# Third edge stage: five of 403 groups fetched row by row through SyncE instead of by GpSimd's gathers

## The reference

```
h = silu(emb @ mlp_w0 + mlp_b0); h = silu(h @ mlp_w1 + mlp_b1)
w = (h @ mlp_w2 + mlp_b2).reshape(-1, 4, MUL)
ss = xs[senders]; vv = xv[senders]
m0 = w[:, 0] * ss
m1 = w[:, 1][:, :, None] * ss[:, :, None] * Y1[:, None, :]
m2 = w[:, 2][:, :, None] * vv
m3 = w[:, 3] * (jnp.einsum('emc,ec->em', vv, Y1) / SQ3)
msg = segment_sum(concatenate(m0, m3, m1, m2), receivers)
```

## Time and profile before

| | |
|---|---|
| median of three runs | 11160.38 us (11138.41 to 11165.17) |
| profiled execution | 11197.17 us, span 11195.4 us |
| busy in the span | PE 7512.2 us, DVE 6853.5, ACT 4365.1, POOL 7061.2 |
| third edge stage | about 5899 to 8612 us |
| DMA in the span | 16 engines, mean 76 GB/s |

### The profile page before, as it was taken

The page is one execution under the profiler, slowest core; times in us unless marked ns, Lnnn a source line. Parts: engine busy times, 40 slices in busy tenths (PEclk is TensorE's granted clock), DMA queues, the critical chain, the costliest instruction groups (busy, mean ns, idle before and its releaser), DMA issues. The chain is left out here.

```text
span 11195.4 us, 158258 instructions
## 1 busy us (share of the span) xinstructions
PE 7512.2 (67%) x45679; PEld 5676.2 (51%) x45679; DVE 6853.5 (61%) x18737; ACT 4365.1 (39%) x7367; POOL 7061.2 (63%) x6167
## 2 busy tenths in 40 slices
PE   1333333335899998998956777777777677777775
PEld 1322322333666666666645666666666344444443
DVE  3555555566677777666655666666666444444445
ACT  1111121121667776666621111111111566666664
POOL 3666666662688888888855555556554655555554
PEclk5555555556889999999977888888888788888887
DMA  4434434442666666777761111111111111111111
GB/s 118 110 96 105 111 98 104 101 97 65 103 106 106 107 106 109 109 109 109 110 117 46 43 43 43 43 42 43 42 42 46 45 43 44 44 44 45 44 44 43
DMA packets 1068830, 846.48 MB, mean 76 GB/s; under 512 B 404136, under 2 KB 907183, under 8 KB 1067542
## 3 DMA queue, kind: packets, MB, share of 16 engines
q0 software_dynamic: 360512, 407.88, 20.9%
q1 hardware_dynamic: 676812, 313.54, 12.7%
q10 hardware_dynamic: 30652, 115.04, 3.1%
HBM read 696.14 MB, written 139.60 MB: 75 GB/s over the span
## 5 line engine op out<-in xcount | busy, mean ns | idle before, releaser
L1474 POOL DMA_INDIRECT sums<-sumrows,index x1460 | 2458.1, 1684 | 694.3 <-issue 348.9
L1623 POOL DMA_INDIRECT rows<-table,index x1612 | 1583.8, 982 | 1128.8 <-DVE mid L1680 582.1
L679 POOL DMA_INDIRECT rows<-table,index x1612 | 1609.3, 998 | 1015.9 <-issue 692.0
L1873 POOL DMA_INDIRECT ACC<-table,index x1472 | 1398.4, 950 | 1129.2 <-DVEq L1998 615.1
L1650 DVE TENSOR_TENSOR ACC<-ACC,psS 128x256 f32 x1612 | 674.6, 418 | 792.1 <-PE psS L1714 471.2
L1714 PEld LDWEIGHTS psS<-hot,mid 128*128 128x128 f32 x6448 | 1042.9, 230 | 57.7 <-issue 3.0
L1714 PE MATMUL psS<-hot,mid 128*128 128x128 f32 x6448 | 1032.2, 313 | 2.7 <-DVE mid L1680 2.3
L2045 PE MATMUL psG<-limbs,pickA 128*128 128x384 bf16 x4060 | 902.1, 355 | 159.4 <-issue 102.7
L1910 ACT ACTIVATE pickA<-apart,K 128x512 bf16<-128x512 bf16 x1015 | 721.2, 711 | 717.2 <-remote 475.0
L1966 DVE TENSOR_TENSOR pickD<-ACC,psK 128x512 bf16<-128x512 f32 x700 | 459.9, 682 | 746.4 <-remote 545.4
L1421 PE MATMUL psB<-pickD,limbs 128*128 128x512 bf16 (+1 forms) x2964 | 824.5, 391 | 81.5 <-DVE pickD L1288 77.0
(11 more groups left out here) (349 smaller groups left out, 15303.0 us busy)
## 6 DMA issues: line engine op xcount, KB each, us to landing
win<-table SPq DMA_DIRECT2D x1612, 64.5 KB
srow<-src_f SPq DMA_DIRECT2D x365, 256.0 KB
HN<-rel_f ACTq DMA_DIRECT2D x102, 512.0 KB
relB<-rel_f ACTq DMA_DIRECT2D x102, 512.0 KB
rows<-table,index POOLq DMA_INDIRECT x3224
er<-limbs SPq DMA_DIRECT2D x1632, 3.0 KB
ACC<-table,index POOLq DMA_INDIRECT x1472
sums<-sumrows,index POOLq DMA_INDIRECT x1460
```

The source lines that it names most:

```text
L679: nc.gpsimd.indirect_dma_start(out=rows[:, r, k, :], out_offset=None, in_=table0[:, :], in_offset=bass.IndirectOffsetOnAxis(ap=index[:, n ...
L1474: nc.gpsimd.indirect_dma_start(out=sums1[u][:, :], in_=sums[:, n % 2, u, :], in_offset=None, compute_op=ALU.add, out_offset=bass.IndirectO ...
L1623: nc.gpsimd.indirect_dma_start(out=rows[:, n % R, u, :], out_offset=None, in_=table2[:, :], in_offset=bass.IndirectOffsetOnAxis(ap=index[: ...
L1873: nc.gpsimd.indirect_dma_start(out=rows[:, n % R, u, :], out_offset=None, in_=table3[:, :], in_offset=bass.IndirectOffsetOnAxis(ap=index[: ...
```

## The change

SP takes over the rows of five groups, numbers 75, 150, 225, 300 and 375 (BYSP); POOL keeps the 398 others (QUICK), over the same four buffers, counted in its own order. SP's loop is written out over the 403 groups. After the load of base it issues its share of the request in hand: 73 steps (SPREAD) for the 512 rows of one group, in 64 batches of 8 (PACE). Before the first batch it loads the 512 source numbers into one partition (`listP`) and waits for them; from the third request on it first waits until the group that last used the buffer is done. A batch reads eight numbers into registers and issues eight DMAs of one row each. The rows go to two buffers of their own (`rowsP`) with a semaphore each, for which DVE waits at those five groups. DVE's other work reads `taken` in place of `rows`. Three semaphores and two tiles are new.

```diff
--- before.py
+++ after.py
@@ -1584,6 +1584,12 @@
                     R = 4
                     last = EDGE_GROUPS - 1
                     index = sb("index2", [P, T], I32)
+                    SPREAD, PACE = 73, 8
+                    BATCH = U * P // PACE
+                    BYSP = [SPREAD + 2 + (SPREAD + 2) * k for k in range(5)]
+                    QUICK = [n for n in range(EDGE_GROUPS) if n not in BYSP]
+                    rowsP = sb("rowsP2", [P, 2, U, C])
+                    listP = sb("listP2", [1, U * P], I32)
                     rows = sb("rows2", [P, R, U, C])
                     base = sb("base2", [2 * NB, R, 2 * P])
                     h1 = sb("h1_2", [P, 2 * P])
@@ -1598,33 +1604,55 @@
                     (s_h0, s_h1, s_h1p, s_h2, s_hot, s_w, s_mid, s_sum, s_free, s_dot, s_dot3, s_q1) = (sem(n + "_e2") for n in (
                         "s_h0", "s_h1", "s_h1p", "s_h2", "s_hot", "s_w", "s_mid", "s_sum", "s_free", "s_dot", "s_dot3", "s_q1"))
                     s_rows = gathered2
+                    s_listP, s_rowsP = sem("s_listP_e2"), sem("s_rowsP_e2", 2)
                     s_index, s_base = sem("s_index_e2"), sem("s_base_e2", R)
                     with nc.Block() as block:
                         @block.sync
                         def _(sp):
                             sp.dma_start(index[:, :], a["src_cols"]).then_inc(s_index, 16)
 
-                            def load(n, g, r):
+                            def eight(b):
+
+                                _, at = nc.values_load_multi_w_load_instructions(
+                                    listP[0:1, b * PACE:b * PACE + PACE], engines=(sp.engine,), min_val=0, max_val=NPAD - 1,
+                                    skip_runtime_bounds_check_because="a src is a node number, and padding edges have one too")
+                                return at
+
+                            for n in range(EDGE_GROUPS):
                                 sp.wait_ge(s_mid, n + 1)
-                                sp.dma_start(base[:, r, :], basis[bass.ds(n * 2 * NB, 2 * NB), :]).then_inc(s_base[r], 16)
-
-                            ring(sp, EDGE_GROUPS, R, load)
+                                sp.dma_start(base[:, n % R, :], basis[n * 2 * NB:(n + 1) * 2 * NB, :]).then_inc(s_base[n % R], 16)
+                                k, step = divmod(n, SPREAD)
+                                if k < len(BYSP):
+                                    for b in range(BATCH * step // SPREAD, BATCH * (step + 1) // SPREAD):
+                                        if b == 0:
+                                            if k > 1:
+                                                sp.wait_ge(s_mid, BYSP[k - 2] + R + 1)
+                                            sp.dma_start(listP.rearrange("o (t p) -> o t p", t=U), a["src_cols"][:, BYSP[k] * U:BYSP[k] * U + U].rearrange("p t -> t p").unsqueeze(0),
+                                                         allow_slow_non_contiguous=True).then_inc(s_listP, 16)
+                                            sp.wait_ge(s_listP, 16 * k + 16)
+                                        at = eight(b)
+                                        for i in range(PACE):
+                                            u, p = divmod(b * PACE + i, P)
+                                            sp.dma_start(rowsP[p:p + 1, k % 2, u, :], table2[bass.ds(at[i], 1), :]).then_inc(s_rowsP[k % 2], 16)
+                            sp.wait_ge(s_index, 16)
+                            for r in range(2):
+                                sp.wait_ge(s_rowsP[r], 16 * U * P * uses(len(BYSP), 2, r))
                             for r in range(R):
                                 sp.wait_ge(s_base[r], 16 * uses(EDGE_GROUPS, R, r))
 
                         @block.gpsimd
                         def _(pool):
                             pool.wait_ge(s_index, 16)
-                            for n in range(EDGE_GROUPS):
-                                pool.wait_ge(s_mid, n + 1)
+                            for f, n in enumerate(QUICK):
+                                pool.wait_ge(s_mid, QUICK[f - R] + R + 1 if f >= R else 1)
                                 pool.nop(nofuse=True)
                                 for u in range(U):
                                     at = n * U + u
                                     nc.gpsimd.indirect_dma_start(
-                                        out=rows[:, n % R, u, :], out_offset=None, in_=table2[:, :],
-                                        in_offset=bass.IndirectOffsetOnAxis(ap=index[:, at:at + 1], axis=0)).then_inc(s_rows[n % R], 16)
+                                        out=rows[:, f % R, u, :], out_offset=None, in_=table2[:, :],
+                                        in_offset=bass.IndirectOffsetOnAxis(ap=index[:, at:at + 1], axis=0)).then_inc(s_rows[f % R], 16)
                             for r in range(R):
-                                pool.wait_ge(s_rows[r], 16 * U * uses(EDGE_GROUPS, R, r))
+                                pool.wait_ge(s_rows[r], 16 * U * uses(len(QUICK), R, r))
 
                         @block.scalar
                         def _(act):
@@ -1653,9 +1681,16 @@
 
                                 s = r % 2
                                 one_hots(hot[:, s, :, :], n).then_inc(s_hot, 1)
-                                dve.wait_ge(s_rows[r], 16 * U * g + 16 * U)
-                                scalars = rows[:, r, :, 0:F]
-                                vectors = rows[:, r, :, F:C].rearrange("p u (c k) -> p u c k", c=3)
+                                if n in BYSP:
+                                    k = BYSP.index(n)
+                                    taken = rowsP[:, k % 2, :, :]
+                                    dve.wait_ge(s_rowsP[k % 2], 16 * U * P * (k // 2 + 1))
+                                else:
+                                    f = QUICK.index(n)
+                                    taken = rows[:, f % R, :, :]
+                                    dve.wait_ge(s_rows[f % R], 16 * U * (f // R) + 16 * U)
+                                scalars = taken[:, :, 0:F]
+                                vectors = taken[:, :, F:C].rearrange("p u (c k) -> p u c k", c=3)
                                 along = unit[:, bass.ds(n * U, U), :].unsqueeze(3).to_broadcast([P, U, 3, F])
                                 m1 = mid[:, s, :, 2 * F:5 * F].rearrange("p u (c k) -> p u c k", c=3)
                                 m2 = mid[:, s, :, 5 * F:8 * F].rearrange("p u (c k) -> p u c k", c=3)
```

## The result

The changed kernel takes 11392.94 us (11387.45 to 11399.67) against 11162.77 us, a ratio of 1.021 with a 95% interval of 1.0192 to 1.0227: 230 us slower, where no change was forecast and 11195 us was the upper end. Its profiled execution took 11387.45 us, span 11385.7.

What follows compares the result with a forecast made beforehand. Third edge stage bound by handovers between PE, ACT and DVE, not POOL's gathers. POOL's relief 0, SP's added work 0, semaphores 0.1 us, bounds -25.6 and +22: 11160 us, no measurable change, range 11125 to 11195.

Steps and rivals of the forecast that it cites:

- bounds of 0 and 22 us for the list: SP's load of 512 source numbers, five times: delay of base costs 0, at most 22 us.
- that idle time hides all of it: SP, third edge stage: 332 us of added work per request of 489, hidden by 1837.8 us of waits; cost 0.
- a wrong releaser: DVE's 260.4 us at line 1650, named as waiting for a load of HN; which semaphore was left open.
- rival B: SP's row loads in each step become the bound, base late, PE waits: 12535 us, mild case 11300; chance 0.07.
- a ring of handovers: Third edge stage: PE, ACT and DVE wait for each other, no engine full; DVE's sums wait 471.2 us, 393 times.
- its own 0.82: Rival B's threshold on SP: it decides above 0.82 us per row; every 0.1 us over costs 256 us.
- the 5.13 at most: SP's step with a batch takes 5.13 us of 6.70; a batch delays the next base by at most that.
- the cover of 9.3 us: SP's base loads: used 13.4 us after issue, issue and landing at most 4.1 us, so 9.3 us spare.
- Rival A: POOL sets the pace where waits do not show: 25.6 us go, 11135 us, -0.23%; chance 0.06.
- C: List or batches on SP make base late beyond the bound, at five places: 11200 us; chance 0.05.
- D: SP's request is not overlapped because each row's DMA is awaited; excluded by the change's text, no chance of its own.
- my 0.6: SP's load of eight row numbers into registers: 0.3 to 0.6 us expected, 0.6 taken.

Runs made afterwards that it cites:

- e6: The changed kernel unaltered, beside the kernel before in a session at the lower level: 15 us faster.
- e20: The changed kernel's list, register loads and row DMAs replaced by 7680 posts, POOL gathering all 403 groups, upper level: 156 us (1.52%) slower than the kernel before.
- e8: The changed kernel with 5632 row DMAs at fixed addresses, no register work, POOL gathering all groups, upper level: 216 us slower than the kernel before.
- e14: Same kernel as e20 (7680 posts, POOL gathering all 403 groups), at the lower level: 0.07 to 0.10% slower than the kernel before.

## Why the prediction was wrong

**Right.** The row loads' medians, 37 + 29 + 228 ns. At the lower level they stood (3.15 - 0.228) / 7 = 0.42 us apart (e6's timeline, forecast 0.516); in the changed kernel itself the median distance within a batch is 0.65 us and the mean 0.70, more than forecast. PE never waited for base beyond the first, the rows came in time, the list cost two waits, 8.2 us of SyncE's and nobody else's; bounds of 0 and 22 us for the list hold with 0. DVE's instructions and POOL's time went as forecast (1583.8 to 1562.6 us, idle up by 246 us).

**The step that failed** is in the part on SyncE: "that idle time hides all of it". I priced SyncE's work by what SyncE has to spare and by who waits for its results. The runs show a third way to pay: at this level, while SyncE issues, the others are released late, and it need not be row loads. e20 shows it with nothing but 7680 posts that nobody reads, 156 us, and e8 with 5632 DMAs at fixed addresses and no register work, 216 us. So the cost I put at 0 was the 230 us. A range by SyncE's spare time could not contain it. How the 230 us divide among the register loads, the register operations, the moves and the DMAs is not shown: the register work was not tried alone at this level.

**Signs that stood in my own rows.** I left a wrong releaser open, 260.4 us at DVE with the name of a load of HN, and passed over the 784.6 us that ACT waited for "remote" in the same view. I saw a load of median 333 ns with single ones of 17853 ns and a stretch of 1.36 us each, and put it down to the load's own 128 pieces, in rival B. The move beside it, with no piece at all, went to 1405 ns in the same stage; had I asked for the line's moves, I would have seen a stop that is not the DMA's. At the lower level the 17.8 us DMA is still there (17789 ns in e6) and the slow moves are not: two things stood under one maximum. And the stage was a ring of handovers with no full engine, where every late handover can delay the next; this is argued, not tested.

**Rival B** had the side and the evidence, but another mechanism: SyncE as the bound, base late. SyncE was held (over the stage, (2922 - 632 - 403 x 0.4 - 320 x 0.714) / 2560 = 0.74 us per row, against 0.43 by the same sum for e6), yet below its own 0.82. Base was issued up to 8.5 us after its release, not the 5.13 at most that I had allowed, but the cover of 9.3 us held, and base was late for nobody. In e20 it was issued 1.9 us late at most, and the loss was there. **Rival A** (-25.6 us) is right at the lower level, where the measured gain is 15 us, interval 2 to 29; at the upper level POOL had 582 us to spare and the relief could not show. C and D did not happen.

**Eight registers in one load** took 0.714 us at the median, not my 0.6. The Trainium skill's figure (Runtime: NRT & Kernel Launch, "Instruction fetch mechanics"), some 200 ns per register, would by estimate be 1.6 us; the measured 0.714 us is 0.09 us per register, so the trace does not agree with it. Eight did cost more than twice four's 0.299 us.

**What holds the engines up is not shown.** The slow moves suggest that the instruction stream itself is stopped. There is a second difference: the trace of the changed kernel holds 104202 semaphore updates at the upper level and, from the same program in e6, 213063 at the lower one; for the posts kernel it is 103420 (e20) against 215453 (e14), while the instructions recorded are nearly as many in both (164841 and 164568 in the whole trace of the change). The Trainium skill (NOTIFIC — the notification-queue block, "Overflow: three behaviours, one of which stalls the engine") says that the path which takes the engines' records of what they did holds the producers back when it is full rather than lose a record inside the block, and that its counter of such stalls, if not zero, would mean that this path had throttled an engine. If that path was full here, the loss would come from the recording, each instruction paying for its record. The stopped moves agree with this; no run read that counter, and the missing updates do not show where they were lost. No run here was made without records, so neither this nor the change's time without them is settled.

## What to carry to other kernels

Idle time of an engine hides added work only if issuing it is free to the others. Look first for the cheapest instructions (register moves, posts) and see whether any takes many times its median: in this case it went with a price of 0.021 to 0.051 us for every instruction added. Before costing a change, check whether the stage is a ring of handovers or has a full engine: here the same change gave +2.1% on the first and -0.17% on the second, from the same program. Measure pairs within one session: levels 18% apart for one kernel can turn the bound of a stage into another. And where an added stream ends before its stage does, compare the stage's pace before and behind its end: it needs no second run.

## What the runs showed of the hardware that I had not expected

One program, two levels (11158 and 9470 us), and the difference is not spread evenly: the first, third and fourth edge stages take 2515.6, 2688.9 and 2441.2 us in the trace of before and 2099, 2025 and 1843 us in e6's, while the second takes 2933 and 2915. In the third stage the medians of the instructions compared are the same at both (PE's sums 275 ns, ACT's silu 473 ns, SyncE's moves 29 ns); the maxima of the cheapest ones are not (register moves 39 against 1380 ns, posts 40 against 1400 ns). The granted clock cannot be the whole difference: in the first edge stage it is 0.56 in the trace of before and 0.57 in e6's, and the times differ by 416 us. In the third it is 0.83 against 0.98, with PE busy for 2070 and 1686 us; whether the lower clock makes the waits there longer or the waits lower the clock is open. At the upper level half of the semaphore updates are missing from the trace, and "remote" or unrelated releasers appear where they are missing.
